# A fused two-layer kernel on one core: VectorE's first splits, x's load and late constants put in another order

## The reference, cut to what matters

```python
# x: (8, 256, 128)   ctx: (8, 512, 128)   16 heads of 8
x = x + xattn_L0(layernorm(x), ctx, ctx, mask)   # softmax(q k / sqrt(8) - 1e9 * mask) v, with biases
x = x + moe_L0(layernorm(x))                     # 32 experts, 8 per token out of 2 of 4 groups, + shared
x = x + xattn_L1(layernorm(x), ctx, ctx)         # the same with rotary positions, no mask
x = x + moe_L1(layernorm(x))                     # 8 experts, 1 per token, + shared
```

## Time and profile before

| | us |
|---|---|
| median of 3 executions | 779.77 |
| lowest and highest | 779.35, 785.31 |
| the profiled execution | 783.57 |
| its span (first to last instruction) | 782.3 |
| busy in the span: PE / DVE / ACT / POOL | 661.6 / 529.5 / 407.7 / 378.6 |

### The profile page before, as it was taken

One profiled execution on the slowest core, in us unless ns is written; L12 is line 12 of the kernel. 1 busy time (PEld: TensorE's weight loads), 2 busy tenths in 40 slices (PEclk: granted clock), 3 DMA queues, 4 the chain that ended last, 5 costly groups with the idle time before them and its releaser, 6 DMA issues.

```text
span 782.3 us, 13823 instructions
## 1 busy us (share of the span) xinstructions
PE 661.6 (85%) x5180; PEld 335.3 (43%) x5180; DVE 529.5 (68%) x922; ACT 407.7 (52%) x550; POOL 378.6 (48%) x559
## 2 busy tenths in 40 slices
PE   4378898989888998999999888888898889686992
PEld 2023333333233666666656333333233224345981
DVE  4487888898987566545555588888888853662332
ACT  2037777777675633332222466766766685532441
POOL 6243556665330356687545547557555111180333
PEclk9559999999996999999999999999999999987996
DMA  6865423542302363756723053374394200013004
GB/s 178 176 222 140 119 80 82 139 120 81 67 2 59 75 165 107 175 139 170 172 81 81 0 138 93 101 192 113 93 205 106 99 3 1 8 41 85 28 28 132
DMA packets 57711, 80.07 MB, mean 102 GB/s; under 512 B 6234, under 2 KB 41834, under 8 KB 55402
## 3 DMA queue, kind: packets, MB, share of 16 engines
q1 hardware_dynamic: 56122, 76.42, 38.0%
q0 software_dynamic: 1248, 2.57, 1.0%
q10 hardware_dynamic: 276, 0.21, 0.1%
HBM read 55.86 MB, written 24.29 MB: 102 GB/s over the span
## 4 chain that ended last, share of the span: by engine, by line
PE 48%; ACT 18%; issue 13%; DVE 10%; DMA 5%; SPq 3%; POOL 3%; DVEq 0%; ACTq 0%; POOLq 0%
ACT prob L808 16%; PE pair L425 10%; PE outs L536 6%; PE pair L305 4%; PE pair L307 4%; PE outs L438 4%; PE pair L306 4%; PE pair L393 3%; PE misc L438 3%; PE misc L351 2%; POOL rows_in L1667 2%; PE outs L334 2%; DVE negmax L1082 2%; PE misc L449 1%; DMA x<-in_x 1%
## 5 line engine op out<-in xcount | busy, mean ns | idle before, releaser
L1082 DVE TENSOR_REDUCE negmax<-pair 128x2 f32<-128x1024 f32 x256 | 307.4, 1215 | 58.8 <-PE pair L393 56.0
L808 ACT ACTIVATE prob<-pair 128x1024 f32<-128x1024 f32 x256 | 260.4, 1025 | 117.6 <-PE pair L425 116.8
L425 PE MATMUL pair<-qstack,kstack 54*128 54x256 bf16 x1024 | 103.0, 280 | 43.9 <-ACT prob L808 42.5
L393 PE MATMUL pair<-kstack,qstack 51*128 51x512 bf16 (+1 forms) x512 | 103.0, 399 | 14.2 <-DVE negmax L1082 7.5
L425 PEld LDWEIGHTS pair<-qstack,kstack 54*128 54x128 bf16 x1024 | 29.8, 95 | 162.5 <-ACT prob L808 124.4
L1288 DVE TENSOR_TENSOR hid<-pair,silu 128x512 f32<-128x512 f32 x68 | 46.7, 688 | 74.2 <-PE pair L307 62.1
L914 ACT ACTIVATE silu<-pair 128x512 f32<-128x512 f32 x68 | 40.6, 599 | 92.9 <-PE pair L307 92.5
L438 PE MATMUL outs<-prob,vaug 128*32 128x256 f32 x1024 | 87.0, 405 | 0.0
L438 PE MATMUL misc<-prob,vaug 128*32 128x256 f32 x1024 | 81.0, 391 | 0.2
L305 PE MATMUL pair<-xT,eh 128*128 128x512 f32 x136 | 71.8, 528 | 0.0
L536 PE MATMUL outs<-hid,down 128*128 128x512 f32 x136 | 69.5, 593 | 0.7 <-POOL hid L1621 0.7
(11 more groups left out here) (259 smaller groups left out, 1063.9 us busy)
## 6 DMA issues: line engine op xcount, KB each, us to landing
kstack<-k_terms SPq DMA_DIRECT2D x32, 384.0 KB
w_here<-w_rows SPq DMA_DIRECT2D x32, 256.0 KB, 4.7
w_there<-w_rows SPq DMA_DIRECT2D x32, 256.0 KB, 4.8
k_terms<-kparts SPq DMA_DIRECT2D x16, 384.0 KB, 2.6
qstack<-q_terms SPq DMA_DIRECT2D x32, 192.0 KB, 3.3
ctx_nat<-in_ctxT SPq DMA_DIRECT2D x16, 256.0 KB, 3.5
k_terms<-kparts SPq DMA_DIRECT2D x16, 256.0 KB, 2.9
w_nat<-in_L_gu SPq DMA_DIRECT2D x3, 1056.0 KB, 5.9
```

The source lines that it names most:

```text
L393: return nc.tensor.matmul(to, qstack[n % 3][rows, g, qt * P:(qt + 1) * P], kstack[n % 3][rows, g, :], start=True, stop=True)
L425: e = nc.tensor.matmul(bank[m + r][:, k * SQ:(k + 1) * SQ], kstack[n % 3][rows, g, (c + k) * P:(c + k + 1) * P], qstack[n % 3][rows, g, :] ...
L808: nc.scalar.activation(prob[:, quad % 2, 2 * g:2 * g + 2, c:c + 2, :].rearrange("p j c q -> p j (c q)"), pair[t_pair(n, step)][:, :, :], A ...
L1082: nc.vector.tensor_reduce(negmax[:, n % 2, 2 * g:2 * g + 2, qt], pair[score_pair(n, step)][:, :, :], AX.X, ALU.max, negate=True).then_inc( ...
```

## The change

Five edits.

1. On VectorE `x_statistics(1)` stands behind `first_keys` and `first_queries`.
2. x is loaded in three pieces: batch 0 as before, batch 1 (128 KB) where the rest stood, and batches 2 to 7 (768 KB) behind `write_k(1)` and ahead of `stack_k(1)`. A semaphore `ld_x1` is added for the middle one.
3. `set_ones(nc.sync, 2)`, the ones of buffer 2, stood behind `stack_q(1)`; now it is in `period(0)`, between `stack_max(0, 1)` and `write_k(2)`.
4. `load_ffn_0` is cut in two: `e_nat` is issued at the end of SP's `period(0)`, the router, the gate bias, `down0` and the two tables at the end of its `period(1)`. `e_nat` has a semaphore of its own, and the counts of `ld_ffn` fall by 16.
5. The two tables no longer stand in the prologue.

```diff
-                    ve.wait_ge(ld_x0 if n == 0 else ld_x, 16)
+                    ve.wait_ge((ld_x0, ld_x1, ld_x)[min(n, 2)], 16)
...
             normalise(0, 0, x_normed_first)
-            x_statistics(1)
             first_keys()
             first_queries()
+            x_statistics(1)
             ve.wait_ge(ld_ident, 16)
...
-                pool.wait_ge(ld_ffn, 64)
+                pool.wait_ge(ld_experts, 16)
...
-            def load_ffn_0():
-                nc.sync.dma_start(rt_nat[:, :], A["L0_router"]).then_inc(ld_ffn, 16)
-                nc.sync.dma_start(gate_bias[:, :], A["L0_ffn_gate_bias"].partition_broadcast(P)).then_inc(ld_ffn, 16)
-                nc.sync.dma_start(e_nat[:, :, :, :], A["L0_gu"]).then_inc(ld_ffn, 16)
-                nc.sync.dma_start(down0[:, :, :], A["L0_down"]).then_inc(ld_ffn, 16)
+            def load_ffn_0(part):
+
+                if part == 0:
+                    nc.sync.dma_start(e_nat[:, :, :, :], A["L0_gu"]).then_inc(ld_experts, 16)
+                else:
+                    nc.sync.dma_start(rt_nat[:, :], A["L0_router"]).then_inc(ld_ffn, 16)
+                    nc.sync.dma_start(gate_bias[:, :], A["L0_ffn_gate_bias"].partition_broadcast(P)).then_inc(ld_ffn, 16)
+                    nc.sync.dma_start(down0[:, :, :], A["L0_down"]).then_inc(ld_ffn, 16)
+                    nc.sync.dma_start(before16[:, :, :], A["c_before"].bitcast(BF16)).then_inc(ld_order, 16)
+                    nc.sync.dma_start(order[:, :], A["c_order"]).then_inc(ld_order, 16)
...
                 n = B * layer + b
-                if b == 0 and layer == 0:
-                    load_ffn_0()
                 if b >= 0:
                     stack_max(n, 1)
+                if b == 0 and layer == 0:
+                    set_ones(nc.sync, 2)
                 if 0 <= b < B - 2:
                     write_k(n + 2)
...
                     stack_q(n + 2)
+                if layer == 0 and 0 <= b < 2:
+                    load_ffn_0(b)
                 if layer and 1 <= b < 6:
...
-            nc.sync.dma_start(x[:, QT:, :], A["x"][:, QT:, :]).then_inc(ld_x, 16)
+            nc.sync.dma_start(x[:, QT:2 * QT, :], A["x"][:, QT:2 * QT, :]).then_inc(ld_x1, 16)
...
             write_k(1)
+            nc.sync.dma_start(x[:, 2 * QT:, :], A["x"][:, 2 * QT:, :]).then_inc(ld_x, 16)
             stack_k(1)
             write_q(1)
             stack_q(1)
-            set_ones(nc.sync, 2)
-            nc.sync.dma_start(before16[:, :, :], A["c_before"].bitcast(BF16)).then_inc(ld_order, 16)
-            nc.sync.dma_start(order[:, :], A["c_order"]).then_inc(ld_order, 16)
```

More of the change, by code:

```diff
@@ L244, in build @@
         rows_out = nc.dram_tensor("rows_out", (T + TILES * P, D), FP32, kind="Internal").ap()
-        ld_x0, ld_x, ld_ident, ld_order = sem("ld_x0"), sem("ld_x"), sem("ld_ident"), sem("ld_order")
+        ld_x0, ld_x1, ld_x, ld_ident, ld_order = sem("ld_x0"), sem("ld_x1"), sem("ld_x"), sem("ld_ident"), sem("ld_order")
         ld_qkv, ld_w, ld_mask, ld_zero = sem("ld_qkv"), sem("ld_w"), sem("ld_mask"), sem("ld_zero")
@@ L254, in build @@
         ld_m = [sem(f"ld_m{i}") for i in range(2)]
-        ld_ffn, ld_empty, w_out = sem("ld_ffn"), sem("ld_empty"), sem("w_out")
+        ld_experts, ld_ffn, ld_empty, w_out = sem("ld_experts"), sem("ld_ffn"), sem("ld_empty"), sem("w_out")
         ld_weight = [sem(f"ld_weight{i}") for i in range(4)]
@@ L629, in shared_down @@
                 fn = FC[c][1]
-                pe.wait_ge(ld_ffn, 224)
+                pe.wait_ge(ld_ffn, 208)
                 pe.wait_ge(su_mul, n + 1)
@@ L850, in period @@
                 if layer == 0 and b == B - 2:
-                    act.wait_ge(ld_ffn, 64)
+                    act.wait_ge(ld_ffn, 48)
                     nc.scalar.activation(rt_w[:, 0, :], rt_nat[:, :], ACT.Copy).then_inc(rt_hi, 1)
@@ L917, in split_gu @@
             def split_gu(u):
-                act.wait_ge(ld_ffn, 224)
+                act.wait_ge(ld_ffn, 208)
                 nc.scalar.activation(gu1[:, u, :, 0, :], w_nat[:, u, :, :], ACT.Copy).then_inc(gu_hi, 1)
```

## The result

The changed kernel took 784.16 us (median of 20 runs, 780.9 to 786.15), the kernel before 781.44 (20 runs on the same chip). The ratio is 1.0034 with a 95% interval of 1.0022 to 1.0047: slower by 0.34%, 2.7 us (1.7 to 3.7). The forecast was no change. The first runs of the kernel before, on which the forecast stood, had a median of 779.77, so of the 4.5 us between 779.7 and 784.16 the change made 2.7 and the base 1.7.

A forecast was written before the change was run, and what follows sets the result against it. Over the first 60 us the chain of waits was taken to run through transfers and SP, not compute. Terms -0.7 - 0.6 + 1.25 came to 0, so the earlier median was carried over: 779.7 us, range 776.9 to 782.5.

The forecast's parts named there:

- The turns: Prologue: VectorE's key splits alternate with POOL's mask work, the last ending at 14.8, 0.7 us earlier than before.
- the rival in which the head comes in full: Prologue: VectorE is not held by POOL, so edit 1 gains 2.1 us; 778.5 in all, chance 0.15.
- Edit 2: costless: Prologue: x in pieces may delay stack_q(1), against 1.4 us of cover; taken as 0, with 1.3 as other end.
- The start of period(0): End of the prologue: period(0) begins 0.7 + 0.6 = 1.3 us earlier.
- The wait for `mT` (0.6): Before period(0): without ones and tables on SP, mT is issued 2.1 us earlier, of which 0.6 count.
- Edit 3 in period(0): Batch 2's first score newly waits for stack_q(2), between 0.7 and 1.8 us; the middle, 1.25, was taken as loss.
- The delay of 2.6 on SP: SP in period(0): four issues of ones put write_k(2) and all behind it 2.6 us later within the period.
- the softening behind `write_q(2)`: SP in period(0): stack_q(2) may follow write_q(2) in 6.4 us as in batch 3, not 7.5, leaving a 0.7 wait.
- the 0.4 + 3.1 taken: stack_q(2) in period(0): its second half is issued some 0.4 us later and lands after 3.1.
- the slack of 0.8: Batch 2's first score: stack_q(2) landed at 75.9, the score ran at 76.72, so 0.8 us of delay is free.
- the slower rival: Batch 2's stacks later through the ones' data in the rings, perhaps a lower TensorE clock; net +2.6, 782.4, chance 0.15.
- The next period: After batch 2's wait: it moves the work behind it, and nothing in the later periods gives it back.

The follow-up runs named there:

- mask_late: Kernel before with VectorE's splits ahead of the statistics, and POOL's mask work held until batch 0's queries are split: 783.04 us in one run.
- loads_only: Kernel before with edits 4 and 5 alone (expert weights and tables loaded late): 777.20 us, ratio 1.0001.
- ones_only: Kernel before with edit 3 alone (ones of buffer 2 between stack_max(0, 1) and write_k(2)): 785.05 us, ratio 1.0052.
- ones_back: Changed kernel with edit 3 undone, the ones of buffer 2 back behind stack_q(1): 781.89 us, ratio 1.0006.
- ones_half: Changed kernel with two of the four issues of ones back behind stack_q(1), two still ahead of write_k(2): 778.29 us, ratio 1.0019.
- changed_keys_first: Changed kernel with write_k(b+2) ahead of stack_max(b, 1) in layer 0, nothing else: 783.08 us, ratio 0.9998.
- warm_wait: Changed kernel with ten more bf16 score matmuls, results unused, ahead of batch 2's first score: 781.55 us, ratio 1.0059.
- split_only: Kernel before with edit 1 alone (VectorE's splits ahead of batch 1's statistics): 780.73 us, ratio 0.999.
- ones_act: Changed kernel with the ones of buffer 2 issued by ScalarE after its prologue and not by SP: 780.61 us, ratio 0.9987.

## Why the prediction was wrong

**Edit 1: right.** The turns gave 14.75 for the forecast 14.8, mask_late shows them by their absence, and the rival in which the head comes in full falls. The Trainium skill's rule on the shared ports (SBUF — State Buffer, "Who interferes with whom") held: VectorE's cast took 1.05 and 1.26 beside POOL and 0.43 without it.

**Edit 2: costless, as taken.** `period(0)` began without a wait for x or for `stack_q(1)`, and from `write_k(1)` to `stack_q(1)` SP took 16.49 us (21.73 to 38.22) against 17.25 before. It was not run alone.

**The start of period(0): right in kind, too small.** 2.74 us and not 1.3. The wait for `mT` (0.6) went as said. The first scores came 1.9 earlier where the splits account for 0.7. The other 1.1 is in the landing of the first stacks, and I can put it down to no edit: loads_only, with VectorE's order unchanged, had its first score at 28.02, 1.4 before the 29.40 of the kernel before. One profile of each is not enough to tell scatter from cause there.

**Edit 3 in period(0): the step that failed.** The prediction said: "I take the middle, **1.25 us**". The cause, the place and the engine that waits were right, and ones_only and ones_back show the cause. The size of this term was wrong, 2.45 for 1.25. The delay of 2.6 on SP came as forecast (2.65), and so did the softening behind `write_q(2)`: it gave 0.71 where I took half of 1.1. Three other things were missing. First, I let TensorE and SP move together through the period. They don't: `stack_max(0, 1)` came 2.35 early, but TensorE was ready for the score at 76.17 - 2.45 = 73.72, 3.0 early, because its steps between them ran 0.65 quicker at the clock that rose sooner, while SP's transfers and issues keep their length. What TensorE gains on SP there turns whole into wait. Second, SP lost another 0.37 between `write_k(2)` and `write_q(2)`, 0.32 of it in the issues of `stack_k(2)` (1.11 against 0.79). Third, the stack took 76.17 - 72.41 = 3.76 from its first issue to the score, against the 0.4 + 3.1 taken, 0.3 more. With the slack of 0.8 as read: 2.65 + 0.37 - 0.71 - 0.8 + 0.65 + 0.3 is about 2.45. The moment at which the clock rises is not the change's work alone: it was at about 60 us before, 56 after and 51 in ones_back, so the 0.65 is that of one profile.

**The clock: known and left out.** The fall behind the wait stood only in the slower rival, at 1.0 us and one chance in seven. It cost 1.53, and it comes wherever there is such a wait: in the changed kernel, ones_back, ones_half, ones_only, loads_only and changed_keys_first. The wait of 1.28 in ones_back was long enough. A wait of that kind should have been costed with it. The short waits ahead of batch 3's first score (0.57 in the changed kernel, 0.74 in ones_only) had L425 at 0.39 behind them, so no fall followed those. The Trainium skill (TensorE: Matmul & The Clock Gate, "HAM oscillation — how this bites in real kernels") has the clock fall over waits of about 3 to 5 us for a transfer between bursts of matmuls; here it fell behind waits of 1.28 to 2.45 too, and warm_wait adds that filling the wait does not always help.

**The next period: wrong.** I said that nothing in later periods gives the wait back, and overlooked that something can be added. Batch 3's first score waited some 0.75 more, where before it had run on time. split_only (0.38) and ones_act (0.72) have this wait too, so it doesn't need the ones. It doesn't need an early `period(1)` either: mask_late waited 0.49 there with `period(1)` at 76.49, as before, and warm_wait, with the ones in place, has no such wait. The three versions with the keys first are free of it. Why it comes in some profiles and not in others is open.

**Edits 4 and 5: right.** 1.0001 for them alone.

Sum with the measured terms: -3.15 + 2.45 + 1.53 + 0.75 is 1.6, the 1.56 that the profiles show at the end of the attention. (By the starts of the rows the wait is 2.6 and not 2.45: the score came 2.84 behind L425 and before 0.24. The rows then go -0.55, +0.98, +1.72 and +1.56.) The runs say 2.7 (1.7 to 3.7). The slower rival, at 0.15, had +2.6; that this lies so near the 2.7 is luck. It had the clock's fall right in kind, 1.0 for 1.53. Its start of `period(0)` was 1.3 early for 2.74, and its reason for the longer wait, the ones' data ahead of `k_terms` in the rings, was not there: the keys took 3.98 us to `stack_k(2)` against 3.93.

**Open.** Why the first stacks land up to 1.4 us earlier in some profiles, and why `stack_q(2)` follows `write_q(2)` by 6.1 to 8.2 us and why TensorE's clock rises anywhere from 50 to 60 us, from one profile to another. Each moves TensorE against SP by about as much as the change does. Also open is whether the gap between the 1.56 of the profiles and the 2.7 of the runs is more than that scatter.

## What to carry to other kernels

Where two sequences run from one point and meet again, here TensorE's steps and one queue's issues, an edit that shortens the one and lengthens the other costs their difference as a wait: work out the slack at the meeting point anew after every term, and never add a gain upstream of it to the sum before asking who else must arrive. Cheap issues (0.46 to 0.81 us each) are dear in the middle of a write, read back, write, read back sequence and cost nothing that showed on a queue with nothing behind it. Shorten that sequence first, then start earlier: the order of two calls on SP and one on VectorE gave 0.5% where five edits had lost 0.3%.

## What the runs showed of the chip

- **Filling a wait did not always keep the clock up.** In the place of a wait of 2.5 us at 2.4 GHz, ten bf16 matmuls over 51 rows (2.32 us, then 0.31 idle) were followed by 1.2 GHz, six fp32 ones over 128 rows (2.84 us) by 2.4 GHz. Rows, type and the time filled changed together, so which of them decides isn't told apart. L334 took 1.22 us against 0.70, L425 0.61 against 0.39.
- **A short wait was enough.** Even a wait of 1.28 us (ones_back) had L425 at 0.61 behind it 2.4 us later; waits of 0.57 and 0.74 (batch 3, the changed kernel and ones_only) had it at 0.39.
- **The price of taking turns.** Four alternating casts and subtractions of 128x512 on VectorE took 4.4 us beside POOL's on 8 partitions and 2.3 us alone.
